# Attention and gated FFN with two layer norms: row maxima turned by a transposing DMA, later turns

## What is computed

```
x  = layernorm(x + attn(x))        # x: 2 x 1024 tokens, 512 wide
x  = layernorm(x + ffn(x))
attn: q, k, v = projections of x, 8 heads, each 8 wide
      softmax(q k^T) / 8 @ v, then @ Wo^T + bo
ffn:  (silu(x @ Wg^T) * (x @ Wu^T)) @ Wd^T
      1792 inner columns; int4 weights with one scale per 128 inputs
```

## Time and profile before

| | |
|---|---|
| median of 3 runs | 515.65 us (515.52 to 516.02) |
| the profiled execution's own time | 515.38 us |
| its span | 513.5 us |
| busy: PE, DVE, ACT, POOL | 499.5, 408.8, 406.8, 282.9 us |
| granted TensorE clock | 0.996 of full speed |

### The profile page before, as it was taken

How to read it: one execution, slowest core, us unless ns; L and a number is a source line. 1 busy time by engine, 2 the same in 40 slices (tenths; PEclk the granted TensorE clock), 3 DMA queues, 4 the chain that set the end, 5 groups by cost and what they waited for, 6 DMA issues and landing times.

```text
span 513.5 us, 8164 instructions
## 1 busy us (share of the span) xinstructions
PE 499.5 (97%) x2986; PEld 194.3 (38%) x2986; DVE 408.8 (80%) x688; ACT 406.8 (79%) x569; POOL 282.9 (55%) x330
## 2 busy tenths in 40 slices
PE   8999999999999999999999999999999999999994
PEld 3222233323333322334444444444444444444441
DVE  2799999989999996478778778778668666788676
ACT  1523889988998889868888888888888888888883
POOL 9200094854744444072664686676885874748741
PEclk9999999999999999999999999999999999999998
DMA  6510018953720007500031121130020020000022
GB/s 194 158 48 19 8 54 210 263 106 73 110 43 2 2 5 164 226 1 0 8 56 21 22 41 22 21 63 1 1 82 1 1 84 0 2 0 1 0 82 82
DMA packets 30151, 29.21 MB, mean 57 GB/s; under 512 B 19488, under 2 KB 21920, under 8 KB 29856
## 3 DMA queue, kind: packets, MB, share of 16 engines
q1 hardware_dynamic: 26544, 22.41, 15.2%
q0 software_dynamic: 3424, 6.03, 6.6%
q10 hardware_dynamic: 144, 0.26, 0.1%
HBM read 24.37 MB, written 4.23 MB: 56 GB/s over the span
## 4 chain that ended last, share of the span: by engine, by line
PE 88%; DVE 5%; ACT 3%; issue 1%; DMA 1%; SPq 0%; POOLq 0%; POOL 0%; DVEq 0%
PE ps L1184 19%; PE ps L1172 19%; PE ps L1263 18%; PE ps L1161 10%; PE ps L1054 8%; PE ps L1132 6%; PE ps L984 3%; ACT pbuf L814 3%; DVE mxh L1361 2%; PE ps L1108 1%; PE ps L1144 1%; DMA arena<-xT 1%; PE ps L1036 1%; PE ps L994 1%; PE ps L1092 1%
## 5 line engine op out<-in xcount | busy, mean ns | idle before, releaser
L1361 DVE TENSOR_REDUCE mxh<-ps 128x1 f32<-128x512 f32 x256 | 157.4, 683 | 4.9 <-PE ps L1054 4.0
L814 ACT ACTIVATE pbuf<-ps,gamma 128x1024 f32<-128x1024 f32 x128 | 137.2, 1115 | 15.4 <-PE ps L1132 12.2
L907 ACT ACTIVATE ps<-ps,ratio 128x512 f32<-128x512 f32 x167 | 105.9, 659 | 41.4 <-PE ps L1172 38.6
L1263 PE MATMUL ps<-wd,stack 128*128 128x512 f16 x440 | 129.7, 379 | 0.0
L1184 PE MATMUL ps<-arena,wu 128*128 128x512 f16 x448 | 115.3, 379 | 0.0
L1172 PE MATMUL ps<-arena,wg 128*128 128x512 f16 x448 | 115.3, 379 | 0.1
L1542 DVE TENSOR_TENSOR ps<-ps,stack 128x512 f32<-128x512 f32 x128 | 87.9, 695 | 32.2 <-PE ps L1263 30.3
L913 ACT ACTIVATE ps<-ps,ratio 128x512 f32<-128x512 f32 x156 | 99.0, 659 | 5.4 <-PE ps L1184 1.1
L709 POOL CAST stack<-pbuf 128x512 f16<-128x512 f32 x55 | 33.5, 609 | 74.4 <-DVE pbuf L1517 74.4
L1542 DVE TENSOR_TENSOR ps<-ps,pbuf 128x512 f32<-128x512 f32 x76 | 52.6, 696 | 23.2 <-PE ps L1263 22.4
L1161 PE MATMUL ps<-pbuf,arena 128*32 128x256 f32 x832 | 66.5, 391 | 0.5 <-ACT avt L821 0.2
(11 more groups left out here) (133 smaller groups left out, 412.7 us busy)
## 6 DMA issues: line engine op xcount, KB each, us to landing
arena<-xT SPq DMA_DIRECT2D x16, 256.0 KB, 5.8
x<-x SPq DMA_DIRECT2D x2, 2048.0 KB, 9.8
out<-x SPq DMA_DIRECT2D x3, 1024.0 KB, 4.2
stack<-down_ratios SPq DMA_DIRECT2D x1, 2048.0 KB, 10.3
wg<-gq POOLq DMA_DIRECT2D x4, 448.0 KB, 8.1
wu<-uq POOLq DMA_DIRECT2D x4, 448.0 KB, 7.4
wd<-dq POOLq DMA_DIRECT2D x2, 896.0 KB, 10.8
pbuf<-down_ratios SPq DMA_DIRECT2D x1, 1536.0 KB, 6.3
```

Of the source, the lines that this page charges most:

```text
L814: nc.scalar.activation(pbuf[:, pi % 4, :].rearrange("p (a n) -> p a n", a=2), ps[:, at:at + 2, :], ACT.Exp, scale=gamma[:, n // (ALL // B) ...
L907: nc.scalar.activation(gbank[t % 2], gbank[t % 2], ACT.Copy, scale=gr[:, t % G, c:c + 1])\
L1263: mm = nc.tensor.matmul(bank[k], mparts[:, a, t % NM, k * P:(k + 1) * P], wd[:, i, :], start=(i == 0 and a == 0), stop=(a == 1), skip_grou ...
L1361: nc.vector.tensor_reduce(mxh[:, f % 2, qh, half:half + 1], ring_bank("first", n), AX.X, ALU.max)\
```

## The change

Seven of the eight turns of maxima (groups 1 to 7) leave PE and ACT. SP turns `mp`, widened to 128 columns, by a transposing DMA into `mrows`, waits for its landing, and issues the same two row transfers. `mp`'s spare columns are set to zero once. The turn of group 0 stays on PE. The avT turns move from step 8f + 9 to 8f + 10; attT moves from step 20 to 22; the two wo turns from 22 and 23 to 23 and 27. Two of block 0's four `add_attention` move on POOL from behind the weight load of iteration f = 3 to between normalise(2) and split_max(4). The waits of `combine` and `split_max` are changed to fit.

```
@@ -281,20 +283,17 @@
-            f, r = divmod(n + 3, KT)
-            if r == 0 and f < NB * NG:
-                return [("M", f, 0)]
-            f, r = divmod(n - 9, KT)
+            f, r = divmod(n - 10, KT)
             if r == 0 and 0 <= f < LASTF:
                 return [("avT", f, 0)]
             r = n - STEPS
-            if r == 4:
+            if r == 6:
                 return [("attT", 0, 0)]
...
-        WO_AT = (6, 7)
+        WO_AT = (7, 11)
@@ -455,7 +454,11 @@
                 if f:
-                    sp.wait_ge(s_read, out_count["M", f, 0])
+                    sp.wait_ge(s_mrow, f + 1)
+                    if f >= 2:
+                        sp.wait_ge(s_mld[g], 16 * 2 * u)
+                    sp.dma_start_transpose(mrows[:, f % 2, :], mp[:, f % 2, :]).then_inc(s_mt, 16)
+                    sp.wait_ge(s_mt, 16 * f)
                 else:
                     sp.wait_ge(s_m0, 1)
@@ -576,9 +581,15 @@
+                if f < 2:
+                    pool.wait_ge(s_pad, 1)
+                elif f == 2:
+                    pool.wait_ge(s_m0, 1)
+                else:
+                    pool.wait_ge(s_mt, 16 * (f - 2))
@@ -679,6 +690,9 @@
             for f in range(2, NB * NG):
                 normalise(f - 2)
+                if f == 4:
+                    for t in range(2, BT):
+                        add_attention(0, t)
                 split_max(f)
...
                 if f == 3:
-                    for t in range(BT):
+                    for t in range(2):
                         add_attention(0, t)
@@ -823,16 +837,8 @@
-            def max_out(f):
-
-                act.wait_ge(s_of, turn_count["M", f, 0])
-                if f >= 2:
-                    act.wait_ge(s_mld[f % NG], 16 * 2 * (f // NG))
-                src = bank[shared_banks("M", f, 0)][0:3 * HG * BT, :].bitcast(F16)[:, 0:P]
-                nc.scalar.activation(mrows[:, f % 2, :], src, ACT.Copy).then_inc(s_read, 1)
@@ -1364,10 +1366,8 @@
             def combine(f):
-                if f == 2:
-                    dve.wait_ge(s_rf, ring_count("M", 0))
-                elif f > 2:
-                    dve.wait_ge(s_of, turn_count["M", f - 2, 0])
+                if f >= 2:
+                    dve.wait_ge(s_mrow, f - 1)
```

More of the change, by code:

```diff
@@ L136, in build @@
         mres = sb("mres", [P, HG * BT], F32)
-        mp = sb("mp", [P, 2, 3 * HG * BT], F16)
-        mrows = sb("mrows", [3 * HG * BT, 2, P], F16)
+        mp = sb("mp", [P, 2, P], F16)
+        mrows = sb("mrows", [P, 2, P], F16)
         ident16 = sb("ident16", [P, P], F16)
@@ L197, in build @@
         s_m0 = sem("first_max_turn_read")
+        s_pad = sem("max_parts_padded")
+        s_mt = sem("max_parts_turned_by_dma")
         s_of = sem("turn_full")
@@ L561, in _ @@
             nc.gpsimd.memset(stack[1][:].bitcast(F32), 0.0).then_inc(s_fill, 1)
+            nc.gpsimd.memset(mp[:].bitcast(F32), 0.0).then_inc(s_pad, 1)
+            pool.wait_ge(s_pad, 1)
             pool.wait_ge(s_fill, 4)
@@ L577, in split_max @@
             def split_max(f):
-                part = [mp[:, f % 2, :].rearrange("p (j i q) -> p i j q", j=2, i=3)[:, i, :, :] for i in range(3)]
+                part = [mp[:, f % 2, 0:3 * HG * BT].rearrange("p (j i q) -> p i j q", j=2, i=3)[:, i, :, :] for i in range(3)]
                 top = mx[:, f % 2, :].rearrange("p (j q) -> p j q", j=2)
                 rest = mres[:].rearrange("p (j q) -> p j q", j=2)
+                if f < 2:
+                    pool.wait_ge(s_pad, 1)
+                elif f == 2:
+                    pool.wait_ge(s_m0, 1)
+                else:
+                    pool.wait_ge(s_mt, 16 * (f - 2))
                 pool.wait_ge(s_mxc, f + 1)
@@ L825, in first_max_out @@
                 act.wait_ge(s_rf, ring_count("M", 0))
-                nc.scalar.activation(mrows[:, 0, :], ring_bank("M", 0)[0:3 * HG * BT, :].bitcast(F16)[:, 0:P],
+                nc.scalar.activation(mrows[0:3 * HG * BT, 0, :], ring_bank("M", 0)[0:3 * HG * BT, :].bitcast(F16)[:, 0:P],
                                      ACT.Copy).then_inc(s_m0, 1)
-            def max_out(f):
-                act.wait_ge(s_of, turn_count["M", f, 0])
-                if f >= 2:
-                    act.wait_ge(s_mld[f % NG], 16 * 2 * (f // NG))
-                src = bank[shared_banks("M", f, 0)][0:3 * HG * BT, :].bitcast(F16)[:, 0:P]
-                nc.scalar.activation(mrows[:, f % 2, :], src, ACT.Copy).then_inc(s_read, 1)
             def wo_out(u, k):
@@ L862, in turn_out @@
                     wo_out(u, k)
-                if kind == "M":
-                    max_out(u)
             act.wait_ge(s_const, 1)
@@ L1055, in first_pass, with turn_first_maxima @@
                                  ks[b][rows, t, half * TB:(half + 1) * TB], start=True, stop=True).then_inc(s_rf, 1)
-            def turn_maxima(f, dst):
-                pe.wait_ge(s_mrow, f + 1)
-                return nc.tensor.transpose(dst[0:3 * HG * BT, :].bitcast(F16)[:, 0:P], mp[:, f % 2, :], ident16[:])
+            def turn_first_maxima(dst):
+                pe.wait_ge(s_mrow, 1)
+                return nc.tensor.transpose(dst[0:3 * HG * BT, :].bitcast(F16)[:, 0:P], mp[:, 0, 0:3 * HG * BT], ident16[:])
             def ring_use(kind, n):
@@ L1071, in ring_use @@
                 else:
-                    turn_maxima(0, ring_bank("M", 0)).then_inc(s_rf, 1)
+                    turn_first_maxima(ring_bank("M", 0)).then_inc(s_rf, 1)
             def turn(kind, u, k):
@@ L1085, in turn @@
                 dst = bank[at]
-                if kind == "M":
-                    mm = turn_maxima(u, dst)
-                elif kind == "avT":
+                if kind == "avT":
                     pe.wait_ge(s_ave, u + 1)
```

## The result

| | before | after |
|---|---|---|
| median of 6 runs each | 515.70 us (515.52 to 516.02) | 518.81 us (516.96 to 519.62) |
| ratio | | 1.0055 (1.0043 to 1.0067) |
| the profiled execution, its span | 515.38, 513.5 us | 518.71, 516.5 us |

The change makes the kernel slower by 0.55%, 3.1 us. The six runs of after are no longer close together as those of before are; two lie at 517 us and four between 518.7 and 519.6. The experiments come back to that.

What follows compares the result with a forecast made beforehand. DVE was taken to set the pace up to 184.7 us. Terms +2.1 (group 2), +0.7 (group 4), -0.9 and -0.2 sum to +1.7 us on 515.38, giving 517.1, taken as 517.2 us; range 514.1 to 519.0.

Steps and rivals of the forecast that it cites:

- Group 2, +2.1: Before scores(16, 0): rows land at 92.5 us behind the load of x, costing DVE 2.1 us; ends 0 and 5.1.
- Behind it on SP's queue: Group 2: the transposing DMA issued at 83.9 us waits for the 2 MB of x ahead on SP's queue.
- bv's 5.7 us: Evidence for queueing: bv, 0.5 KB behind the loads of x transposed, takes 5.7 us; 28 KB alone take 1.8.
- Group 4, +0.7: Before scores(32, 0): rows at 133.15 us against 132.65 less 0.2, so 0.7 us late; ends 0.1 and 1.4.
- Removal of the M turns, 0: Seven turns of maxima leave PE and ACT: none has a DVE gap beside it, so removal gains 0.
- avT a step later, -0.9: Six avT turns, each with a 0.21 us DVE gap: moving them gains 0.9 us; at most 1.26, at least 0.
- wo apart, -0.2: Two wo turns four steps apart: only the third gap of 0.16 us and little more goes; ends 0 and -1.0.
- the fourth rival: Step 27's wo turn still collides with step 26's avT and av's evacuation; worth +-0.3 us, inside other cases, no own chance.
- The transposing DMA, 2.4 us: In each group's chain before its scores: the 32 KB transposing DMA with landing takes 2.4 us.
- the prediction's larger estimate, 3.3 us: Transposing DMA time from two Trainium skill figures added; would make group 4 1.6 us late and the sum 1.2 us higher.
- a cover of 0.9: Groups 1, 3, 5 and 6: 7.7 us from combine to scores, 6.8 needed, so cost 0 with 0.9 us spare.
- Drain and FFN, 0: After 214.5 us the stage only moves as a block; group 7 costs 0, or 0.1 with the slower end.

Runs made afterwards that it cites:

- the second copy: The changed kernel measured again with nothing changed, beside the kernel before: 519.57 us, ratio 1.0072.
- the kernel that keeps PE busy: The changed kernel with ten useless 128 x 512 products on PE ahead of the wait for group 2's rows: 517.05 us, ratio 1.0027.
- x early: The changed kernel with the first 2 MB load of x issued ahead of max_rows(1), about 51 us, instead of at 80: 514.64 us, ratio 0.9985.
- the two copies: The changed kernel measured a second and a third time, nothing changed: 519.57 us (1.0072) and 518.88 us (1.0063).
- the DMA twice: The changed kernel with x loaded early and each group's transposing DMA done twice, one after the other: 530.35 us, ratio 1.0289, two runs.
- x on ACT's queue: The changed kernel with the first load of x issued by ACT instead of SP at the same moment: 518.34 us, ratio 1.0057.
- x in halves: The changed kernel with the first load of x split into two of 1 MB, the second behind max_rows(2): 519.39 us, ratio 1.0075.

## Why the prediction was right and where it was wrong

The direction, the place and the range held: 517.2 us was forecast within 514.1 to 519.0, and 518.81 was measured. The range held by little: the second copy's median, 519.57, lies above it. Two of the six runs, 516.96 and 517.25, lie on the forecast, and so does the kernel that keeps PE busy, 517.05. The profiled one, 518.71, has the forecast's gap and in place of the clock's loss the late start of 1.4 us. Term by term:

- **Group 2, +2.1.** Measured 2.19 us in the first trace, 2.87 and 3.05 in the two others, of which 0.4 and 0.2 us are the slow clock at the first products behind the wait. The rows went out at 91.05, 89.6 without the late start, where 89.5 was forecast. The mechanism was half right. It rests on the load of x, as x early shows. "Behind it on SP's queue" is wrong: on ACT's queue the load holds it as long. The row that I leaned on, bv's 5.7 us, does not tell a queue's order from full engines.
- **The TensorE clock: the missing term, +1.8.** The forecast counted the wait in front of the scores and stopped there. In eight of the eleven runs of the two copies the mean clock is below that of before, and in the traces that wait is then followed by a stretch at 0.50 of the clock, at which PE, not DVE, sets the pace. Of the traces, the second and third of the changed kernel and the one with the DMA twice show it, the first of the changed kernel does not (its mean clock is that of before, 0.996). The test is PE kept busy, which takes 1.8 us off the median; in the two traces that show the drop it cost 2.5 and 1.3 us.
- **Group 4, +0.7.** Measured 0, but only just: rows issued at 132.90, landed at 135.86, when the POOL load that waits for them starts, scores(32, 0) at 135.90 in the trace. Counted from group 4's `combine`, POOL finished 0.2 us earlier and the scores came 0.3 later than I had them; the chain took 0.2 us less.
- **Removal of the M turns, 0.** Measured -0.9 to -1.0. "None has a DVE gap beside it" was read from brackets alone. The cost was in the length of the runs of reductions (13.37 against 13.27 us for 22) and in the wo gap one step on, which I took for the cost of a single turn.
- **avT a step later, -0.9, and wo apart, -0.2.** Measured 0. The six gaps shrank from 0.21 to 0.16 or 0.17 only, and group 4's `combine` lost as much. That a wo turn's 0.83 belongs to the single turn was wrong: with nothing in the step ahead it is 0.45. At its new places each wo turn again stands one step behind another, attT and avT, and so both gaps stayed; the fourth rival named the second of these.
- **The transposing DMA, 2.4 us.** 2.3 to 2.4 for groups 1, 4, 6 and 7, so the prediction's larger estimate, 3.3 us, is not borne out. Groups 3 and 5 needed 4.4 and 3.9 in the first trace, 2.0 and 1.5 more than the forecast had, against a cover of 0.9. Group 3's cost nothing that shows. Group 5's held PE for 0.20 us, in no bracket of DVE: its 26 reductions took 15.84 us, where groups 4 and 6 took 15.65.
- **Drain and FFN, 0.** 328.9 us both times.

The two gains that were wrong nearly cancel: -1.1 was forecast for moved turns and -0.9 came from the removed ones. Group 2 with its clock kept cost 2.5 us of the stretch (166.44 less 163.93), 0.4 over its term, and group 4's 0.7 did not come. So the sum without the clock, 1.7 us in both, was right partly by luck.

The kernel with the early load of x keeps the gain and loses the cost: 514.64 us, 0.9985 (0.9976 to 0.9994) of before. The gain is small, 0.15% with 0.06% as the near end of its interval. So the change was sound and what it lacked was one line at another place.

## What to carry to other kernels

A transfer that enters a chain with a deadline has to be costed with the bytes under way at its moment, on any queue; look in the trace for the bulk loads of that stretch before asking how long it takes alone, and move those; splitting one here only moved the collision. A wait on TensorE has a second price, the clock behind it, so count it separately and look at the granted clock after each new wait. A cost hidden in the mean length of a pipelined run shows in no bracket: compare the run's length per instruction at places with and without the edit. And before a gap is called the cost of a single turn, look at a place where no other turn stands near it.

## What the hardware showed

- After waits of PE of 2.59 and 2.96 us the granted clock was 0.50 for some 6 and 3 us, and it fell to 0.50 after 1.95 us too (the DMA twice, group 4). In other executions, after 2.33, 2.74 and 3.03 us (after; x on ACT's queue; x in halves, group 3), it stayed at 1.00. So the length of the wait alone does not decide, and what does was not settled.
- A transposing DMA of 32 KB mostly takes 1.1 to 1.2 us of SP to issue and lands in 2.3 to 2.4 us alone; with 2 MB under way 5.8 to 6.6.
- Group 5's took 3.4 to 4.2 us in the traces, with a DMA share between 0.00 and 0.20 after its issue in the first. Of other transfers only one fetch of instructions, 16 KB, stands in that stretch; POOL's bias addition runs from 149.28 to 153.82 us over it. The cause stays open.
